# The skip term D*u and the silu(z) gate of a selective scan move to TensorE and VectorE

## What is computed

```python
xz = h @ in_proj_w                       # h: normalised input, 256 features; 2 x 512 columns
x, z = jnp.split(xz, 2, axis=-1)         # 512 channels each
x = silu(causal_depthwise_conv(x, conv_w, conv_b))      # called u below
xp = x @ x_proj_w                        # 64 columns for delta, 16 B, 16 C
delta = softplus(xp[..., :64] @ dt_proj_w + dt_proj_b)
# for each channel d and state n, over time t (16 states per channel):
#   h[t] = exp(delta[t] * A[d, n]) * h[t-1] + delta[t] * B[t, n] * u[t]
#   y[t] = sum over n of h[t] * C[t, n]
y = y + u * D_param                      # the skip term
y = y * silu(z)                          # the gate
out = y @ out_proj_w
```

## Time and profile before

| | |
|---|---|
| median of 3 runs | 3341.56 us (3336.74 to 3346.06) |
| the profiled execution | 3336.77 us, its span 3334.9 us |
| PE busy | 2692.5 us (81%) |
| DVE busy | 2665.0 us (80%) |
| ACT busy | 1683.3 us (50%) |
| POOL busy | 2242.9 us (67%) |
| mean granted clock of TensorE | 0.869 of full speed |

### The profile page before, as it was taken

The page is one execution under the profiler, slowest core; times in us unless marked ns, Lnnn a source line. Parts: engine busy times, 40 slices in busy tenths (PEclk is TensorE's granted clock), DMA queues, the critical chain, the costliest instruction groups (busy, mean ns, idle before and its releaser), DMA issues. The chain is left out here.

```text
span 3334.9 us, 33308 instructions
## 1 busy us (share of the span) xinstructions
PE 2692.5 (81%) x10093; PEld 1368.5 (41%) x10093; DVE 2665.0 (80%) x2530; ACT 1683.3 (50%) x2327; POOL 2242.9 (67%) x1251
## 2 busy tenths in 40 slices
PE   3999999767868778768768768768877657999998
PEld 1555656543414314314315314314312124556565
DVE  6777777309998998988998988998999956777774
ACT  2444444246665665655665655665664513444442
POOL 4555554218888877878887877878878844556552
PEclk9999999887978968968968968968966569999999
DMA  3011000018776875876875776775866820000100
GB/s 101 20 32 32 31 26 22 29 35 193 170 181 157 184 174 147 185 164 155 184 181 141 185 166 155 182 172 154 191 167 158 200 84 31 29 29 32 31 26 19
DMA packets 164631, 379.72 MB, mean 114 GB/s; under 512 B 21990, under 2 KB 81446, under 8 KB 164198
## 3 DMA queue, kind: packets, MB, share of 16 engines
q1 hardware_dynamic: 146678, 358.67, 44.0%
q10 hardware_dynamic: 17776, 18.94, 2.0%
HBM read 308.26 MB, written 44.11 MB: 106 GB/s over the span
## 5 line engine op out<-in xcount | busy, mean ns | idle before, releaser
L927 POOL TENSOR_TENSOR mix_scan<-mix_scan,mix_bc 128x1024 f32<-128x1024 f32 x512 | 1204.8, 2359 | 379.1 <-DVE mix_scan L1092 378.4
L1092 DVE TENSOR_TENSOR_SCAN mix_scan<-mix_decay,mix_ps_du 128x1024 f32<-128x1024 f32 x512 | 1169.7, 2285 | 68.8 <-ACT mix_decay L1043 26.5
L1229 PE MATMUL mix_ps_du<-mix_stack,mix_sel 96*128 96x512 bf16 x1024 | 377.8, 458 | 462.9 <-DVE mix_scan L1092 429.5
L1108 DVE TENSOR_TENSOR mix_ps_du<-mix_ps_du,mix_bc 128x1024 f32<-128x1024 f32 x512 | 618.1, 1207 | 97.5 <-PE mix_ps_du L1229 84.8
L647 PE MATMUL ffn_ps_gate_up<-ffn_w_gate_up,ffn_xT 128*128 128x512 f32 (+1 forms) x1536 | 663.2, 569 | 14.6 <-DVE ffn_h L454 13.1
L1043 ACT ACTIVATE mix_decay<-mix_decay,mix_a_neg 128x1024 f32<-128x1024 f32 x512 | 572.4, 1143 | 130.7 <-DMA mix_decay<-delta_rows 129.9
L1229 PEld LDWEIGHTS mix_ps_du<-mix_stack,mix_sel 96*128 96x128 bf16 x1024 | 75.0, 103 | 829.3 <-DVE mix_scan L1092 712.1
L677 PE MATMUL ffn_ps_down<-ffn_w_down,ffn_hT 128*128 128x256 f32 (+1 forms) x1536 | 386.3, 394 | 11.4 <-ACT ffn_hT L582 11.4
L647 PEld LDWEIGHTS ffn_ps_gate_up<-ffn_w_gate_up,ffn_xT 128*128 128x128 f32 x1536 | 273.6, 191 | 282.1 <-issue 231.8
L1214 PE MATMUL mix_ps_y<-mix_scan,mix_red 128*32 128x512 f32 x2048 | 354.5, 776 | 5.3 <-POOL mix_scan L927 5.3
L454 DVE TENSOR_TENSOR ffn_h<-ffn_silu_gate,ffn_ps_gate_up 128x704 f32<-128x704 f32 x128 | 113.7, 888 | 303.4 <-ACT ffn_silu_gate L587 303.4
(11 more groups left out here) (129 smaller groups left out, 3501.0 us busy)
## 6 DMA issues: line engine op xcount, KB each, us to landing
mix_decay<-delta_rows SPq DMA_DIRECT2D x512, 512.0 KB, 7.5
mix_stack<-mix_parts SPq DMA_DIRECT2D x384, 64.0 KB, 2.0
delta_rows<-mix_delta SPq DMA_DIRECT2D x32, 512.0 KB, 3.1
ffn_x<-_attn_hidden_states_dram SPq DMA_DIRECT2D x32, 256.0 KB, 2.9
after_ffn<-ffn_y SPq DMA_DIRECT2D x32, 256.0 KB, 3.0
mix_x_tokens<-after_ffn SPq DMA_DIRECT2D x32, 256.0 KB, 7.2
mix_x_residual<-after_ffn ACTq DMA_DIRECT2D x32, 256.0 KB, 5.4
...
```

Of the source, the lines that this page charges most:

```text
L927: G.tensor_tensor(wt, wt, bc[:, r % 2, 1, :], ALU.mult).then_inc(hc_done, 1)
L1092: V.tensor_tensor_scan(w[:, slot % RING, :], da[:, slot % SPREADS, :], ps_du[:, slot % 2, :], 0.0, ALU.mult, ALU.add).then_inc(scan_done, 1)
L1108: V.tensor_tensor(ps_du[:, slot % 2, :], ps_du[:, slot % 2, :], bc[:, r % 2, 0, :], ALU.mult)\
L1229: ins = M(ps_du[:, slot % 2, h * 512:(h + 1) * 512], const.sel[0:SEL, i, :], stack[:, c % 2, q, h * 512:(h + 1) * 512], start=True, stop=True)
```

## The change

The skip term is no longer added by DVE. TensorE has a third kind of matmul in the accumulation of `ps_y`: after the last quad of a chunk, for each half, it multiplies a diagonal matrix with D_param (`d_diag`, 128 x 128, made by ACT in the preparation) with `u` (512 columns, 32 bit) and adds the result to the sums. DVE then multiplies `ps_y` by silu(z) at s = 4 and writes the finished `u`; POOL's multiplication at s = 5 is gone, and with it the semaphore `y_taken`. DVE now also waits there for `zs`, and PE waits for `yg_done`, raised by DVE, where it waited for `y_taken`.

```diff
--- before.py
+++ after.py
@@ -94,6 +94,7 @@
         self.aneg = a.sb("a_neg", [P, DI // NCH])
 
         self.conv_diag = a.sb("conv_diag", [P, CHUNKS, TAPS, P])
+        self.d_diag = a.sb("d_diag", [P, CHUNKS, P])
         self.sel = a.sb("sel", [P, 4, P], BF16)
         self.sel_bc = a.sb("sel_bc", [P, 2, P])
         self.red = a.sb("red", [P, 4, 4, NCH])
@@ -293,6 +294,7 @@
                                      alog[:, :].rearrange("g (d n) -> g n d", d=NCH), ACT.Copy)\
                   .then_inc(alog_sorted, 1)
                 for c in range(CHUNKS):
+                    nc.scalar.activation(const.d_diag[:, c, :], ident[:, :], ACT.Copy, scale=const.dpar[:, c:c + 1])
                     for t in range(TAPS):
                         nc.scalar.activation(const.conv_diag[:, c, t, :], ident[:, :], ACT.Copy,
                                              scale=const.cw[:, c, t:t + 1])
@@ -794,7 +796,7 @@
         spread_in = [S(f"delta_spread{k}") for k in range(SPREADS)]
         rep_du = S("rep_du")
         exp_done, dbu_done, scan_done, hc_done = S("exp_done"), S("dbu_done"), S("scan_done"), S("hc_done")
-        y_made, y_taken, yg_done = S("y_made"), S("y_taken"), S("gate_done")
+        y_made, yg_done = S("y_made"), S("gate_done")
         res_in, out_stored = [S(f"res_in{k}") for k in range(4)], [S(f"out_stored{k}") for k in range(4)]
 
         block = ctx.enter_context(nc.Block())
@@ -925,14 +927,6 @@
                         pool.wait_ge(scan_done, R * 64 + (slot + 1))
                         wt = w[:, slot % RING, :]
                         G.tensor_tensor(wt, wt, bc[:, r % 2, 1, :], ALU.mult).then_inc(hc_done, 1)
-                    gated = core(r, full) if c > 0 else (full or r >= 1)
-                    if s == GATE + 1 and gated:
-                        b, cc = (R, c - 1) if c > 0 else (R - 1, 3)
-                        par = (r if c > 0 else r - 1) % 2
-                        pool.wait_ge(y_taken, chunk(b, cc))
-                        pool.wait_ge(taken["Z"], chunk(b, cc) * 2)
-                        G.tensor_tensor(u[:, par, cc, :], u[:, par, cc, :], zs[:, cc % 2, :], ALU.mult)\
-                         .then_inc(yg_done, 1)
                     b, cc = (R, c + 1) if c < 3 else (R + 1, 0)
                     par = (r if c < 3 else r + 1) % 2
                     if (c < 3 and core(r, full)) or (c == 3 and nxt):
@@ -1113,8 +1107,8 @@
                     par = (r if c > 0 else r - 1) % 2
                     if s == GATE and gated:
                         dve.wait_ge(y_made, chunk(b, cc) * 4)
-                        V.scalar_tensor_tensor(u[:, par, cc, :], u[:, par, cc, :], const.dpar[:, cc:cc + 1], ps_y[:, :],
-                                               ALU.mult, ALU.add).then_inc(y_taken, 1)
+                        dve.wait_ge(taken["Z"], chunk(b, cc) * 2)
+                        V.tensor_tensor(u[:, par, cc, :], ps_y[:, :], zs[:, cc % 2, :], ALU.mult).then_inc(yg_done, 1)
                     for sl, kind, rel, k, bank, _ in job_list(r, full):
                         if kind == "O" and sl == slot - 1:
                             dve.wait_ge(made["O"], nth("O", R - 1, k))
@@ -1207,13 +1201,16 @@
                 c, i = divmod(m, 4)
                 y = ps_y[:, h * 512:(h + 1) * 512]
                 if i == 0 and h == 0 and (m > 0 or r > 0):
-                    pe.wait_ge(y_taken, R * 4 + c)
+                    pe.wait_ge(yg_done, R * 4 + c)
                 if h == 0:
                     pe.wait_ge(hc_done, R * 64 + 4 * (m + 1))
                 for q in range(4):
                     ins = M(y[32 * q:32 * q + 32, :], const.red[:, i, :, :].rearrange("p a b -> p (a b)"),
                             w[:, (4 * m + q) % RING, h * 512:(h + 1) * 512],
-                            start=(i == 0), stop=(i == 3), skip_group_check=True)
+                            start=(i == 0), stop=False, skip_group_check=True)
+                if i == 3:
+                    ins = M(y, const.d_diag[:, c, :], u[:, r % 2, c, h * 512:(h + 1) * 512],
+                            start=False, stop=True, skip_group_check=True)
                 if h == 1:
                     ins.then_inc(y_made, 1)
 
```

## The result

| | before | after |
|---|---|---|
| median of 20 runs | 3339.9 us (3336.2 to 3350.6) | 3331.3 us (3328.5 to 3342.8) |
| ratio, with its 95% interval | 1 | 0.9975 [0.9967, 0.9982] |
| span of the profiled execution | 3334.9 us | 3329.3 us |
| mean granted clock of TensorE | 0.869 | 0.884 |

The changed kernel is 8.6 us faster by the medians, 0.25%. It was timed again, as a control, with the same outcome: 0.9979 [0.997, 0.9989].

A forecast was written before the change was run, and what follows sets the result against it. DVE was taken to set the pace, so only its work and waits count. Terms -1 - 14 + 7 - 2.5 + 9 = -1.5 us, from 3341.6 to 3340 us, called no change; range 3323 to 3357 us.

The forecast's parts named there:

- What bounds the kernel: Mixer: DVE sets the pace at 3.49 us a slot; the change acts only through DVE's work and its idle places.
- DVE's gate, -1: DVE's 32 gate instructions, 1273 ns each, become products near 1207 ns: at most 2.1 us less, taken as -1 us.
- Slot 8, -14: Output projection O 0 no longer waits for POOL's late gate: gain 7.5 to 20 us, taken as -14 us.
- Slots 2/3, 0: Added matmuls where DVE has no wait for PE and PE pauses: 0, up to 0.3 us a batch.
- Slots 18/19, +7: First half's matmul delays job P 2, ACT and DVE's wait at slot 22: 7 x 1.0 = +7 us; second half hides.
- Slots 34/35, -2.5: Matmuls half fill PE's pause, delaying C 10 and C 11 or keeping the clock up: -5 to +11, taken as -2.5 us.
- Slots 50/51, +9: PE late at low clock in four batches: added matmuls cost 0 to 15 us, taken as 2.2 us each, +9 us.
- After the last scan, 0: 2.5 us before O 0 go, two added matmuls of 2.0 or 3.8 us come: -0.5 to +1.3, taken as 0.
- The signs: Right: slot 8 wait near 3 us, slot 22 about 1 us longer; wrong: slot 52 over 5 us, new waits at 4 or 20.
- PE's queue becomes the bound: Slots 50/51: PE has no pause and the clock never rises, +19.5, 3361 us; chance 0.2 for over +10 us.
- The filled pauses keep the clock up: Slot 8 gives 20, slot 37 gives 5, slot 50 costs nothing: -19, 3323 us; chance 0.24 for over -10 us.
- POOL's relief is worth nothing: Another wait behind POOL's gate at slot 7 would remove the 14 us: +12.5, 3354 us; part of the slower cases (0.20).

The follow-up runs named there:

- e1: Kernel before, with POOL's gate multiplication issued ahead of its product of slot 5, no added matmuls: ratio 0.9963, 3329.7 us.
- e4: Kernel after with the diagonal matmuls of chunk 2 only (slots 50/51), skip term of the other chunks left out: ratio 0.9979, 3329.4 us.
- e2: Kernel after without any diagonal matmul, skip term left out, DVE still multiplying by silu(z): ratio 0.9941, 3319.3 us.
- e5: Kernel after without the diagonal matmuls of chunk 2 (slots 50/51), that chunk's skip term left out: ratio 1.0001, 3342.5 us.

## Why the forecast of no change held, and which of its terms didn't

*What bounds the kernel.* Right. DVE sets the pace. The 72 us taken off POOL show in the time only where PE waits for the gate; e1 has the gain at slot 8 with POOL's work unchanged.

*DVE's gate, -1.* Measured 40.7 to 38.9 us, -1.8.

*Slot 8, -14.* Right in size and cause, 35.6 to 21.1 us. The early gate on POOL alone gives the same 21.1, and the diagonals without it leave 33.2. "What is late next is O 0 itself" holds as well. The far end of 20 us, O 0 wholly at the high clock, wasn't reached: 4.07 us for its records in batch 2 against 3.72. What I had not followed is that slots 10 to 12 take 2.7 us of it back (5.4 between the second executions).

*Slots 2/3, 0.* Measured +2.3 us at slot 4. The sum is near the bound of 7 x 0.3 us, but it is 0.76 us in each of three batches, over twice the bound for one.

*Slots 18/19, +7.* The chain that I named is right: P 2 starts one diagonal later and ACT's wait grows by 0.95 us. Its price is right too where like is compared with like: 0.91 us at slot 21 in batches where the clock stayed high at slots 15 to 17. But slots 20 to 23 rose by 10.9 us in all. I had followed only ACT's decay to slot 22. The second half's matmul, which I let "hide behind ACT", stands in front of the gate of slot 20 in the batches where PE is already late (+3.0). And a low spell of 3.4 us moved onto the jobs in front of the replicate for slot 23 (+4.9), a cost of the clock that the term didn't have. Moving the diagonal took back 13.9 us.

*Slots 34/35, -2.5.* Right, by the mechanism given as its near end: -3.8 at slot 37, +1.8 at slots 34 to 36, -2.0 together. Taking the diagonals out of that pause brought the low clock and 10.0 us back.

*Slots 50/51, +9.* This is the step that failed: measured -8.5 us. One end was 15 us, with the clock low in four batches whatever is put behind it and both diagonals passing through whole at 1.9 us; I took 2.2 of these 3.8 us a batch. In the profile after, the delta job ahead of them already runs at 2.4 GHz (1.98 us), and the diagonals take about 1.1 us. I had named the other end ("dense matmuls may lift the clock") and put it at 0; the profile showed room below 0, since the waits of 9.5 us could go altogether. That rule of the Trainium skill, "TensorE: Matmul & The Clock Gate", section "What's actually happening", which says that activity releases the low clock, was the better guide at this place than the present durations of the earlier trace rows. The trace agrees with it where the diagonal stands (3.77 to 1.98 us behind it), but it doesn't tell why e4 keeps 15.2 us of waits.

*After the last scan, 0.* Measured -0.7 us. DVE waits 9.61 us for the sums instead of 6.2, and O 0 follows the gate by 1.4 us:

```profile
2710.67 2.08 PE L1212 MATMUL mix_ps_y<-mix_u,mix_d_diag 128*128 128x512 f32 x2
...
2715.94 1.23 DVE L1111 TENSOR_TENSOR mix_u<-mix_ps_y,mix_silu_z 128x1024 f32<-128x1024 f32 x1 [9.61 <-PE mix_ps_y L1212]
...
2717.31 14.05 PE L1194 MATMUL mix_ps_job<-mix_w_out,mix_u 128*128 128x256 f32 x64 [1.41 <-DVE mix_u L1111]
```

*The sum.* The idle times were forecast to change by -0.5 us in all and changed by -8.5: slot 50 came out 17.5 us below its term, while slots 18 to 23 came out 3.9 above, slots 10 to 12 2.7, slot 4 2.3, slot 48 0.6 and slots 34 to 37 0.5. That the time stayed within the band of 10 us is in part luck: the one large miss was more than halved by smaller ones the other way. The places don't give the time to the microsecond either. The profiled executions differ by 5.6 us and the medians by 8.6, against the 1.5 forecast, and the median before was itself 1.7 us below the one that I had started from.

My diagonals cost 7 - 2.5 + 9 = 13.5 us in the loop and nothing net behind it, and the experiment without them says 12. That agreement is luck: by the places of the first table they cost -8.5 + 14.5 = 6 us in the loop, and by the trace of e2 7.6, with another 3.7 behind the last scan. At slots 21/22 the kernel before has 19.8 us where e2 has 15.4, since its clock was low at slots 15 to 17 in four batches and that of e2 in one.

*The signs.* Slot 8, the wait for the gate, the diagonals' 1.0 us and the gate's 1.21 us came as listed under right. The longer wait came at slot 21 instead of 22. Of the signs listed under wrong, new waits at slots 4 and 20 did come, 2.3 and 3.0 us in sum; those at slot 52 didn't.

*The rivals.* "PE's queue becomes the bound" happened at slot 52 with chunk 2's diagonals alone (15.2 us), not in the change. "The filled pauses keep the clock up" was right at slots 37 and 52 and would have given 3323 us. Slot 52 gained 8.5 us more than it says. But slot 8 gave 14.5 us and not 20, slots 20 to 23 cost 3.9 more, and slots 4, 10 to 12, 34 to 37 and 48 together 8.6 more, so the time stayed 8 us above. "POOL's relief is worth nothing" is refuted by e1.

*Open.* Why the clock stays up at slot 49 in the kernel after and falls there in e4 and in three batches of e5; why it falls at slots 15 to 17 in some batches and not in others, behind the same pause of 1.63 us; and how far the places of PE's work in time decide it.
